# Mixing products with 128 rows instead of 64, a PSUM bank per two time blocks, in an attention and feed-forward kernel

## What is computed

```python
def cond(x, condition, weights):            # x (128, 32, 512), weights (16, 32, 32)
    W = weights[condition]
    return jnp.einsum('bct,bcd->bdt', x, W)

q_c = hidden @ Wq_c.T + bq_c                # hidden = cond(...), 512 positions contracted
kv  = hidden @ Wkv_c.T + bkv_c
...
x = x + attn(cond(x, itok_B_0_15, cond_weights), ...)
x = x + ffn(cond2(x, itok_B_8_3872, ...), ...)
```

## Time and profile before

| | us |
|---|---|
| median of three runs | 785.07 |
| lowest, highest | 785.02, 785.12 |
| the profiled execution | 785.16 |
| its span, first to last instruction | 783.4 |

### The profile page before, as it was taken

The page is one execution under the profiler, slowest core; times in us unless marked ns, Lnnn a source line. Parts: engine busy times, 40 slices in busy tenths (PEclk is TensorE's granted clock), DMA queues, the critical chain, the costliest instruction groups (busy, mean ns, idle before and its releaser), DMA issues.

```text
span 783.4 us, 18621 instructions
## 1 busy us (share of the span) xinstructions
PE 758.1 (97%) x7821; PEld 599.0 (76%) x7821; DVE 617.0 (79%) x1109; ACT 377.4 (48%) x675; POOL 199.1 (25%) x203
## 2 busy tenths in 40 slices
PE   7999999999999999999999999999999699999996
PEld 5776777778677767868686777778676599999996
DVE  4476789988998786778777766968888578888887
ACT  2375546455563675565454636445674322222221
POOL 5002020011002000262200000000042388888871
PEclk9899999999999999999999999999999899999999
DMA  9910010010002000000400010002206159899861
GB/s 230 238 49 5 2 59 2 1 31 30 2 2 59 1 2 2 28 2 10 90 3 2 2 55 2 2 2 58 82 2 184 65 127 201 204 202 205 203 132 69
DMA packets 42739, 51.74 MB, mean 66 GB/s; under 512 B 7024, under 2 KB 29600, under 8 KB 42656
## 3 DMA queue, kind: packets, MB, share of 16 engines
q1 hardware_dynamic: 40384, 49.87, 25.9%
q0 software_dynamic: 1056, 0.49, 0.3%
q10 hardware_dynamic: 1216, 0.19, 0.1%
HBM read 41.91 MB, written 8.63 MB: 65 GB/s over the span
## 4 chain that ended last, share of the span: by engine, by line
PE 90%; DVE 5%; ACT 3%; issue 2%; another core or an unknown queue 1%; POOL 0%; DVEq 0%
PE ps L730 33%; PE ps L599 9%; PE ps L600 8%; PE ps L601 8%; PE ps L778 7%; PE ps L797 4%; PE ps L1063 4%; PE ps L1064 4%; PE ps L616 3%; PE ps L1032 2%; PE ps L693 1%; DVE z_low L1423 1%; PE ps L1020 1%; PE ps L1022 1%; PE ps L1021 1%
## 5 line engine op out<-in xcount | busy, mean ns | idle before, releaser
L1163 ACT ACTIVATE qt<-ps,m_bias 128x512 f32<-128x512 f32 x228 | 145.5, 684 | 96.4 <-PE ps L730 96.4
L730 PE MATMUL ps<-q_high,m_high 64*128 64x512 f32 x768 | 154.5, 398 | 2.4 <-ACT qt L1163 1.3
L730 PE MATMUL ps<-q_high,m_low 64*128 64x512 f32 x768 | 150.8, 388 | 0.0
L730 PE MATMUL ps<-q_low,m_high 64*128 64x512 f32 x768 | 108.3, 387 | 0.0
L1423 DVE TENSOR_TENSOR z_low<-ps,z_high 128x512 fp32r<-128x512 f32 x128 | 79.7, 682 | 15.9 <-ACT z_high L1182 15.9
L730 PEld LDWEIGHTS ps<-q_high,m_high 64*128 64x128 f32 x768 | 72.6, 184 | 24.5 <-issue 8.7
L730 PEld LDWEIGHTS ps<-q_low,m_high 64*128 64x128 f32 x768 | 72.7, 184 | 14.7
L529 POOL TENSOR_TENSOR o_sum<-o_part,o_part 128x512 f32<-128x512 f32 x7 | 9.1, 1303 | 294.0 <-ACT o_part L1192 294.0
L730 PEld LDWEIGHTS ps<-q_high,m_low 64*128 64x128 f32 x768 | 72.7, 185 | 13.6
L1182 ACT CAST z_high<-ps 128x512 fp32r<-128x512 f32 x128 | 66.8, 597 | 22.9 <-PE ps L797 22.9
L1168 ACT ACTIVATE sc<-sc 128x512 f32<-128x512 f32 x60 | 37.3, 631 | 46.6 <-DVE sc L1408 41.1
(11 more groups left out here) (292 smaller groups left out, 1646.0 us busy)
## 6 DMA issues: line engine op xcount, KB each, us to landing
x_in<-in_x SPq DMA_DIRECT2D x16, 512.0 KB, 3.6
x_s<-in_x SPq DMA_DIRECT2D x32, 256.0 KB, 5.7
out<-res SPq DMA_DIRECT2D x31, 256.0 KB, 3.6
toep_high<-taps_scratch SPq DMA_DIRECT2D x32, 192.0 KB, 4.3
toep_low<-taps_scratch SPq DMA_DIRECT2D x32, 192.0 KB, 5.0
toep_far<-taps_scratch SPq DMA_DIRECT2D x32, 64.0 KB, 5.5
wq_nope<-in_L_attn_Wq_up SPq DMA_DIRECT2D x2, 768.0 KB, 10.1
wq_nope<-in_L_attn_Wq_up SPq DMA_DIRECT2D x1, 1536.0 KB, 16.3
```

Of the source, the lines that this page charges most:

```text
L730: mm = pe.matmul(ps[:, fold_bank(u, j) + e, :], weights[rows, (GH * g + j) // 2, c, :], moving[c][rows, :], start=start, stop=stop)
L1163: act.activation(qt[:, j, :], ps[:, fold_bank(u, j) + j % 2, :], ACT.Identity, bias=m_bias[:, h:h + 1]).then_inc(s["qt_done"], 1)
```

## The change

One product for each time block and group takes the place of two: it contracts all 128 partitions with the whole 128 x 128 matrix, so a step has 8 products of 128 moving columns instead of 16 of 64. The bank now depends on the time block: blocks 0 and 1 go to the first bank of a step, 2 and 3 to the second, and `h_ready` rises when each is full. The copies and subtractions read a whole bank and write two whole time blocks of the tile, without the 64-column pieces. `project_ca` waits for three of the tile's four subtractions ahead of time block 0 and for the fourth ahead of block 2. What is stored in `h_high` and `h_low`, and how many copies, subtractions and signals there are, stays.

```diff
-    h_of = lambda tile, i, e: (tile[:, i % 2].rearrange("p t (g e c) -> p e t g c", g=2, e=2)[:, e])
-    h_bank = lambda i, e: ps[:, MIX_BANK(i, e), :].rearrange("p (t g c) -> p t g c", t=TT, g=2)
...
-                for tt in range(TT):
-                    for g in range(2):
-                        for e in range(2):
-                            rows, o = slice(64 * e, 64 * e + 64), tt * P + 64 * g
-                            mm = pe.matmul(ps[:, MIX_BANK(i, e), o:o + 64], x_in[i % 2][rows, g, tt * P:(tt + 1) * P],
-                                           mix_of(i)[rows, g, rows], start=True, stop=True)
-                            if tt == TT - 1 and g == 1:
-                                mm.then_inc(s["h_ready"], 1)
+                for n in range(2):
+                    for t_ in range(2):
+                        for g in range(2):
+                            tt = 2 * n + t_
+                            o = t_ * HT + g * P
+                            mm = pe.matmul(ps[:, MIX_BANK(i, n), o:o + P], x_in[i % 2][:, g, tt * P:(tt + 1) * P],
+                                           mix_of(i)[:, g, :], start=True, stop=True)
+                    mm.then_inc(s["h_ready"], 1)
 
             def project_ca(k):
                 if k == 0:
                     pe.wait_ge(s["wcT_done"], 2)
-                pe.wait_ge(s["h_low_done"], 4 * k + 4)
                 for tt in range(TT):
+                    if tt % 2 == 0:
+                        pe.wait_ge(s["h_low_done"], 4 * k + 3 + tt // 2)
...
             def mixed_high(i):
-                for e in range(2):
-                    act.wait_ge(s["h_ready"], 2 * i + e + 1)
-                    act.copy(h_of(h_high, i, e), h_bank(i, e)).then_inc(s["h_high_done"], 1)
+                for n in range(2):
+                    act.wait_ge(s["h_ready"], 2 * i + n + 1)
+                    act.copy(h_high[:, i % 2, 2 * n:2 * n + 2, :].rearrange("p a n -> p (a n)"),
+                             ps[:, MIX_BANK(i, n), :]).then_inc(s["h_high_done"], 1)
...
             def mixed_low(i):
-                for e in range(2):
-                    dve.wait_ge(s["h_high_done"], 2 * i + e + 1)
-                    dve.tensor_tensor(h_of(h_low, i, e), h_bank(i, e), f(h_of(h_high, i, e)),
+                for n in range(2):
+                    dve.wait_ge(s["h_high_done"], 2 * i + n + 1)
+                    dve.tensor_tensor(h_low[:, i % 2, 2 * n:2 * n + 2, :].rearrange("p a n -> p (a n)"),
+                                      ps[:, MIX_BANK(i, n), :],
+                                      f(h_high[:, i % 2, 2 * n:2 * n + 2, :].rearrange("p a n -> p (a n)")),
                                       ALU.subtract).then_inc(s["h_low_done"], 1)
```

## The result

| | before | after |
|---|---|---|
| median, us | 785.05 | 776.24 |
| lowest, highest | 784.43, 785.12 | 774.90, 777.40 |
| the profiled execution's span | 783.4 | 773.1 |
| its mean granted clock (1 = 2.4 GHz) | 0.989 | 0.997 |

A forecast was written before the change was run, and what follows sets the result against it. TensorE, busy for 97% of the span, was taken to bound the kernel: 785.16 - 2.6 (rounds) - 0.35 (start) = 782.2 us profiled, 782.1 median. Own range 781.3 to 782.9 (0.66); 780.0 to 784.2 at a little over 8 in 10.

The forecast's parts named there:

- The rounds: Seven rounds of two mixings: same pitch, 0.111 us, but cheaper edges; 0.37 us less each, 2.6 us in all.
- B: Rival, chance 0.04: moving columns set the mixing's pace, so a round grows by 3.6 us; +25 us, 810.
- A: Rival, chance 0.12: nothing gained at the rounds' edges, as the entry step belongs to semaphore waits; 784.5 us.
- The evictions: ACT's copies and DVE's subtractions: lengths unchanged within 0.02 us each, earlier starts, no gain for PE.
- The start: From the first mixings to the projections: split wait lets PE begin 0.62 us sooner, worth 0.35 us at the end.
- That PE spends less time in the first two mixings is worth nothing: Start: ACT began at 16.3 us, while the first mixing's records end at 13.77; gain nothing.
- The wait in two parts: Start of the projections: first six products go after the third subtraction, 0.62 us sooner, hiding the fourth.
- The clock: Start: half clock from 18.8 to 25.6 us; if the rise stays, 0.33 us gained, if it moves along, 0.62.
- Rival C: Chance 0.10: at the start, fewer records shift ACT's hold or the clock rises sooner; up to 2.5 us more, 779.6 to 781.
- Rival D: Chance 0.08: half clock from 609.3 to 616.1 us falls otherwise over the work, up to 2.4 us either way; 783.5.

The follow-up runs named there:

- e5: Changed kernel, but the two mixings of the start use 128 rows and 64 columns, as many records as before the change; 781.31 us, ratio 0.9961 to the kernel before.
- e1: Kernel before with the new form and split wait only in the two mixings of the start, rounds old; 779.84 us, ratio 0.9936.
- e2: Kernel before with the new form only in the seven rounds, start and whole wait old; 782.90 us, ratio 0.9973.
- e4: Changed kernel with both signals of a mixing given after its last product; 778.69 us, against 785.19 for the kernel before.
- e3: Changed kernel with one wait for all four subtractions ahead of the projections; 779.33 us, against 785.19 for the kernel before.
- e16: Kernel before, unedited, run and profiled again in a later batch; 783.49 us, ratio 1.0007.
- e13: Kernel before with new rounds, old start, and GpSimd's gathers of mixing weights waiting for the four start signals; 780.19 us, ratio 0.9995.
- e12: Changed kernel, unedited, run again in a later batch; 777.09 us, ratio 0.9904 to the kernel before.
- e17: Changed kernel, unedited, run again in the last batch; 776.10 us, ratio 0.9913 to the kernel before.
- e6: Kernel before with new rounds, old start, but there all products of one row half before the other's; 785.30 us, ratio 1.0001.

## Why the prediction came out too small

**The rounds: right.** Forecast 0.37 us a round and 2.6 in all; measured 0.35 and 2.4. The pitch was 0.111, and B fell: 64 and 128 columns come at one pitch (e5). A fell as well: the step at the entry went with the rows, though the waits stayed. The Trainium skill's rule that a change of tiling mode drains TensorE ("TensorEngine Tiling (Array Packing)", Key Properties) agrees: 4.38 us with the two changes and 4.03 without, in e1 and e2 too. Its other rule, to tile the rows when 64 or fewer are contracted (When to Use Tiling), does not pay here, where a product of half the rows and columns costs its pair the same 0.112 us.

**The evictions: right.** Still 0.58 to 0.59 and 0.69 us, and no round waits for them.

**The start: the step that failed.** Three things in one term:
- "That PE spends less time in the first two mixings is worth nothing". I had ACT's 16.3 as a fixed time, because PE's records were done 2.5 us before. The rows said only that something unnamed held it; a wait without a name has no known length in the new kernel. e4 shows that the signal half a mixing sooner is worth 1.6 to 2.5 us.
- The wait in two parts was priced at 0.62 us, the length of a subtraction in a row of four. With the banks filled one after the other the subtractions are 0.89 apart or more, so it is 0.84 us without the hold. In e3 and in after, with it, the fourth signal came 1.49 and 1.45 us behind the third.
- The clock. I let it fall at 18.8 as before, and asked only when it would rise. But it fell there while PE waited for the subtractions, and the change takes most of that wait away. That is 2.83 us in the profiled pair. It would have come without the hold too: e16 has the half clock. (A wait of this kind doesn't always bring it: e13 had the old start and no half clock behind it.) In all, 0.35 stands against 6.2 measured.

**Rival C was the case.** It named both causes, the hold and the clock, but as "or", at up to 2.5 us and with a chance of 0.10. They came together, 3.37 and 2.83 us, and the range's lower end of 780.0 had room for one. Its mechanisms were not the ones that the runs show: half as many records aren't needed (e5 has as many as before, and its first signal was prompt), and the clock didn't rise sooner, it didn't fall.

**Rival D** had its share: 3.4 us less half clock near 600, 1.7 us, on the side of the gain in this profiled pair. In e12 it was not there.

What stays open: why PE's signals were held in the first batches, and why in the new form it was mostly those of step 1 that were late, by 0.1 to 0.9 us against e17, with one of step 0 in after, by 0.4, and in e5, by 1.0.

## What to carry to other kernels

Before a term is put at nothing because "the next engine started later anyway", name what that engine waited for; if no row names it, take the whole unexplained stretch into the range. When a change shortens or removes a stretch in which PE is nearly idle, price the half clock that follows it as well: here the products at 0.43 instead of 0.23 us cost 2.8 us, beside 3.1 for the later start. For short fp32 products with a weight load each, up to 128 columns wide, count the records, not rows or columns (that it is the load that sets their pitch was not tested), and put neighbours of the same row count beside each other.

## What the runs showed of the hardware that was not expected

- The clock can fall while PE has no gap at all: e6 ran 64-row products one at a time, one every 0.112 us, and fell to half at 14.4 us in their midst, in one trace; e5 ran 128-row products at the same pitch and kept the full clock.
- The pitch of these fp32 products is 0.11 us with 32, 64 and 128 moving columns at full clock, and 0.213 at half (64 columns, e6).
- One and the same kernel had medians of 784.75 to 785.19 us in four batches (runs from 783.1 to 786.1) and ran at 779.6 to 785.0 in two. In the profiled executions of the latter all signals were prompt, and the time went roughly with the mean granted clock, 780 us at 0.997 and 783.4 to 785.0 at 0.989.
